# Attention on one Trainium2 core: the result kept transposed up to the output projection, normalised on GpSimd with sums turned through DRAM

## The reference

```
B, S, D, H, HD = 8, 1024, 256, 16, 16
h    = layernorm(x) * (1 + ca) + sa                    # modulation from silu(c) @ wmod
q    = h @ W_q;  latent = (h @ W_k + h @ W_v) @ W_down_kv
k, v = latent @ W_up_k, latent @ W_up_v                # 16 heads of 16
s    = (q_h @ k_h^T) / sqrt(D) * exp(-0.01 |t - t'|)
x    = x + ga * (softmax(s) @ v_h, heads joined) @ W_o
h    = layernorm(x) * (1 + cb) + sb
x    = x + gb * fp4_linear(silu(fp4_linear(h, w_gate)) * fp4_linear(h, w_up), w_down)
```

## Time and profile before

| | us |
|---|---|
| median of 3 runs | 2778.95 (2777.27 to 2779.09) |
| span of the profiled execution | 2775.7 |
| PE busy | 2597.7 (94%) |
| DVE busy | 2345.5 (85%) |
| ACT busy | 1601.3 (58%) |
| POOL busy | 970.2 (35%) |

### The profile page before, as it was taken

One profiled execution on the slowest core, in us unless ns is written; L12 is line 12 of the kernel. 1 busy time (PEld: TensorE's weight loads), 2 busy tenths in 40 slices (PEclk: granted clock), 3 DMA queues, 4 the chain that ended last, 5 costly groups with the idle time before them and its releaser, 6 DMA issues. The chain is left out here.

```text
span 2775.7 us, 54634 instructions
## 1 busy us (share of the span) xinstructions
PE 2597.7 (94%) x15110; PEld 1209.7 (44%) x15110; DVE 2345.5 (85%) x4659; ACT 1601.3 (58%) x2988; POOL 970.2 (35%) x865
## 2 busy tenths in 40 slices
PE   5887679999999999999999999999978999999998
PEld 3333213343444444344344344443323566666665
DVE  5888698888888888888888888888756999999997
ACT  3666507777777777777777777777762222222221
POOL 3666522122122122122122122122231555555654
PEclk8767659999999999999999999999997999999999
DMA  4777864446455455455456455456201111111110
GB/s 152 246 247 255 265 129 73 71 74 99 62 85 87 63 82 82 71 78 86 70 78 86 72 80 86 69 79 94 39 11 38 37 41 40 40 40 42 40 32 18
DMA packets 207121, 238.56 MB, mean 86 GB/s; under 512 B 32256, under 2 KB 150784, under 8 KB 206720
## 3 DMA queue, kind: packets, MB, share of 16 engines
q1 hardware_dynamic: 194560, 218.56, 40.7%
q0 software_dynamic: 3072, 8.39, 1.2%
q10 hardware_dynamic: 9216, 8.39, 0.9%
HBM read 149.79 MB, written 83.89 MB: 84 GB/s over the span
## 5 line engine op out<-in xcount | busy, mean ns | idle before, releaser
L856 DVE CUSTOM_DVE_ANT_0 unread<-max_ps,toeplitz_sb 128x1024 bf16<-128x1024 f32 x1024 | 1219.2, 1219 | 230.5 <-PE max_ps L689 221.9
L817 ACT ACTIVATE probs<-score_ps 128x512 f32<-128x512 f32 x2048 | 1113.3, 597 | 438.3 <-PE score_ps L722 299.7
L689 PE MATMUL max_ps<-k_low,q_low 96*128 96x512 bf16 x2048 | 717.5, 393 | 30.0 <-DVE ident_bf L847 17.9
L651 POOL TENSOR_TENSOR probs<-probs,up_probs 128x512 f32<-128x512 f32 x256 | 336.8, 1316 | 624.4 <-ACT up_probs L821 624.4
L750 PE MATMUL pv_ps<-probs,v 128*32 128x512 f32 x4096 | 548.9, 608 | 3.4 <-POOL probs L651 3.4
L722 PE MATMUL score_ps<-q_low,k_low 99*128 99x512 bf16 (+3 forms) x1280 | 407.9, 320 | 4.9 <-ACT probs L817 4.1
L714 PE MATMUL score_ps<-q_up,k_up 99*128 99x512 bf16 (+3 forms) x1280 | 408.0, 319 | 4.5 <-ACT probs L817 3.8
L1284 PE MATMUL gu_ps<-wgu_t,turned 128*128 128x512 f32 (+1 forms) x768 | 314.7, 559 | 0.6 <-DVE hid L1445 0.6
L657 POOL DMA_DIRECT2D attn<-out_n x64 | 48.8, 762 | 698.3 <-DVE out_n L920 674.8
L714 PEld LDWEIGHTS score_ps<-q_up,k_up 99*128 99x128 bf16 x1280 | 123.8, 97 | 350.4 <-ACT probs L817 325.2
L689 PEld LDWEIGHTS max_ps<-k_low,q_low 96*128 96x128 bf16 x2048 | 194.0, 99 | 156.5 <-DVE row_max L856 83.9
(11 more groups left out here) (145 smaller groups left out, 3218.2 us busy)
## 6 DMA issues: line engine op xcount, KB each, us to landing
splits<-parts SPq DMA_DIRECT2D x128, 384.0 KB, 2.6
q_low<-splits SPq DMA_DIRECT2D x192, 128.0 KB, 4.4
k_low<-splits SPq DMA_DIRECT2D x192, 128.0 KB, 7.0
q_up<-splits SPq DMA_DIRECT2D x192, 128.0 KB, 9.4
k_up<-splits SPq DMA_DIRECT2D x192, 128.0 KB, 12.0
v_padded<-v_out SPq DMA_DIRECT2D x64, 256.0 KB, 3.5
v<-v_padded SPq DMA_DIRECT2D x32, 512.0 KB, 13.9
x_in<-in_L_attn_x SPq DMA_DIRECT2D x16, 512.0 KB, 4.6
```

The costliest lines, as they stand in the source:

```text
L651: nc.gpsimd.tensor_tensor(probs[:, g % PROBS, :, at:at + P], probs[:, g % PROBS, :, at:at + P], up_probs[:, g % 2], ALU.add).then_inc(diag ...
L689: mm = pe.matmul(max_ps[:, i % 2, half * HALF:(half + 1) * HALF], low[0][u][0:KROWS, h, qb * P:(qb + 1) * P], low[1][u][0:KROWS, h, half * ...
L817: nc.scalar.activation(probs[:, g % PROBS, h, :], score_ps[:, i % 2, :], ACT.Exp).then_inc(exp_done, 1)
L856: nc.vector.tensor_tensor_reduce(unread[:, i % 2, :], max_ps[:, i % 2, :], toeplitz[:, at:at + S], 1.0, -3.0e38, ALU.mult, ALU.max, row_ma ...
```

## The change

The product of a half is no longer turned. `out_t` has two buffers, one a half. SP moves the four rows of sums to DRAM and back as 128 partitions x 16 (`turn_sums`), DVE inverts them there (`invert`, at the end of g = 6 for half 1 of the unit before, of g = 14 for half 0), SP moves the inverses to DRAM and back spread over all 32 rows of each head (`spread_inverse`), and POOL multiplies 128x512 in place (`normalise`: after its fourth diagonal addition for half 1 of the unit before, after its last for half 0). SP stores the result head by head to `attn_t` (four DMAs of 32 KB a half). The feed stage loads its tiles from `attn_t` as the left operand of the projection; its transposes of the attention result and that pipeline stage are gone.

```diff
@@ attention, SP
+        def turn_sums(b, u, hf):
+            n = 2 * (UNITS * b + u) + hf
+            sp.wait_ge(out_copied, n + 1)
+            sp.dma_start(t["sums"][hf], out_t[HD:P:VW, hf, :]).then_inc(sums_stored, 16)
+            sp.wait_ge(sums_stored, 16 * (n + 1))
+            sp.dma_start(sums[:, hf, :], t["sums"][hf].rearrange("h (a c) -> (h a) c", a=P // UH)
+                         ).then_inc(sums_loaded, 16)
+        def spread_inverse(b, u, hf):
+            n = 2 * (UNITS * b + u) + hf
+            sp.wait_ge(inverted, n + 1)
+            sp.dma_start(t["inverse"][hf].rearrange("h (a c) -> (h a) c", a=P // UH), inverse[:, hf, :]
+                         ).then_inc(inverse_stored, 16)
+            sp.wait_ge(inverse_stored, 16 * (n + 1))
+            sp.dma_start(inverse_rows[:, hf, :], t["inverse"][hf].unsqueeze(1).broadcast_to(
+                [UH, VW, HALF])).then_inc(inverse_loaded, 16)
+        def store_out(b, u, hf):
+            sp.wait_ge(out_normal, 2 * (UNITS * b + u) + hf + 1)
+            for h in range(UH):
+                sp.dma_start(t["attn_t"][b, u * UH + h, :, hf * HALF:(hf + 1) * HALF],
+                             out_t[h * VW:h * VW + HD, hf, :]).then_inc(out_stored[hf], 16)
         def step(b, u, last):
             ...
                 load_low(b if u < 2 else b + 1, (u + 2) % UNITS)
             if not (last and u == UNITS - 1):
                 load_up(b if u < UNITS - 1 else b + 1, (u + 1) % UNITS)
+            if not (isinstance(unit, int) and unit == 0):
+                before = (b if u > 0 else b - 1, (u - 1) % UNITS)
+                store_out(*before, 0)
+                turn_sums(*before, 1)
+                spread_inverse(*before, 1)
+                store_out(*before, 1)
+            turn_sums(b, u, 0)
+            if not (last and u == UNITS - 1):
                 load_max_rows(unit + 1, (u + 1) % UNITS)
+            spread_inverse(b, u, 0)
@@ attention, POOL
-            pool.dma_start(t["attn"][b, hf * HALF:(hf + 1) * HALF, ...], out_n[:]...)
+        def normalise(b, u, hf):
+            count = held(pool, 16 * (2 * (UNITS * b + u) + hf + 1))
+            pool.wait_ge(minus_ones_set, UNITS + 2)
+            pool.wait_ge(inverse_loaded, count)
+            nc.gpsimd.tensor_tensor(out_t[:, hf, :], out_t[:, hf, :], inverse_rows[:, hf, :],
+                                    ALU.mult).then_inc(out_normal, 1)
@@ attention, PE
-            for c in range(DIAG):
-                mm = pe.transpose(side_ps[:, c, :], out_t[:, c * P:(c + 1) * P], w["ident"][:])
-            mm.then_inc(out_turned, 1)
@@ attention, ACT
-            act.wait_ge(out_turned, n)
+            if not (isinstance(unit, int) and unit == 0):
+                act.wait_ge(out_stored[hf], 16 * OUT_STORES * unit)
@@ attention, DVE
-            nc.vector.reciprocal(inv_sum[:], turned[:, :, :, HD]).then_inc(inv_ready, 1)
-            nc.vector.tensor_tensor(out_n[:], turned[:, :, :, 0:HD], ...)
+            dve.wait_ge(sums_loaded, count)
+            nc.vector.reciprocal(inverse[:, hf, :], sums[:, hf, :]).then_inc(inverted, 1)
...
+                if g == 6 and not (isinstance(unit, int) and unit == 0):
+                    invert(b if u > 0 else b - 1, (u - 1) % UNITS, 1)
+                if g == 14:
+                    invert(b, u, 0)
@@ feed
-            sp.dma_start(attn_in[i % 4][:], t["attn"][b, i * P:(i + 1) * P, :]).then_inc(tile_loaded[i % 4], 16)
+            sp.dma_start(attn_in[i % 4][:], t["attn_t"][b, :, :, tokens].rearrange(
+                "(k h) d s -> (h d) k s", k=DC)).then_inc(tile_loaded[i % 4], 16)
-                mm = pe.matmul(out_ps[:, 0:D], turned[i % 2][:, k, :], w["wo_g"][:, b, k, :],
+                mm = pe.matmul(out_ps[:, 0:D], attn_in[i % 4][:, k, :], w["wo_g"][:, b, k, :],
-                mm = pe.transpose(turn_ps[:, k * P:(k + 1) * P], attn_in[i % 4][:, k * P:(k + 1) * P], w["ident"][:])
```

More of the change, by code:

```diff
@@ L636, in _ @@
             step(B - 1, u, True)
+        store_out(B - 1, UNITS - 1, 0)
+        turn_sums(B - 1, UNITS - 1, 1)
+        spread_inverse(B - 1, UNITS - 1, 1)
+        store_out(B - 1, UNITS - 1, 1)
+        for i in range(2):
+            sp.wait_ge(out_stored[i], 16 * OUT_STORES * UNITS * B)
     @block.gpsimd
@@ L724, in scores, with up_diagonals @@
             mm.then_inc(scores_ready, 1)
-        def up_diagonals(b, u, g):
+        def up_diagonals(b, u, g, last):
             unit, kb = UNITS * b + u, g % TILES
             ks = slice(kb * P, (kb + 1) * P)
-            if g == TILES + DIAG:
-                pe.wait_ge(out_ready, 2 * unit + 1)
+            if g == TILES + DIAG and not last:
+                pe.wait_ge(max_turn_copied, unit + 2)
             pe.wait_ge(up_limited, diagonals_before(unit, g))
@@ L775, in unit_steps @@
                     if h == 1 and is_diagonal(g):
-                        up_diagonals(b, u, g)
+                        up_diagonals(b, u, g, last)
                 if not (first and g < LAG):
                     values(*steps_back(b, u, g, LAG))
-                if g == 5 and not first:
-                    turn_out(2 * unit - 1)
                 if g == 9 and not last:
                     turn_maxima(unit + 1)
-                if g == 10:
-                    turn_out(2 * unit, 0 if last else unit + 2)
         def max_tiles(u, n):
@@ L804, in _, with copy_out @@
             values(B - 1, UNITS - 1, g)
-        turn_out(2 * UNITS * B - 1)
     @block.scalar
     def _(act):
-        def copy_out(n):
-            act.wait_ge(pv_done, TILES * (n + 1))
-            act.wait_ge(out_turned, n)
-            nc.scalar.activation(out_t[:], pv_ps[:], ACT.Copy).then_inc(out_copied, 1)
+        def copy_out(unit, hf):
+            act.wait_ge(pv_done, TILES * (2 * unit + hf + 1))
+            if not (isinstance(unit, int) and unit == 0):
+                act.wait_ge(out_stored[hf], 16 * OUT_STORES * unit)
+            nc.scalar.activation(out_t[:, hf, :], pv_ps[:], ACT.Copy).then_inc(out_copied, 1)
         def exp(unit, g, h):
@@ L908, in round_weights, with unit_steps @@
                               weight_scale).then_inc(weight_step, 1)
-        turned = side_ps[:].rearrange("p c (h r) -> p c h r", r=VW)
-        def invert_sums(n):
-            dve.wait_ge(out_turned, n + 1)
-            nc.vector.reciprocal(inv_sum[:], turned[:, :, :, HD]).then_inc(inv_ready, 1)
[L916 to L924, removed]
+        def unit_steps(b, u, last):
             unit = UNITS * b + u
@@ L931, in unit_steps @@
                         maxima(ahead[0], ahead[1], ahead[2] + i)
[L933 to L936, removed]
                     if not last and (g, i) in SPLIT_AT:
@@ L1158, in sem @@
         return st.enter_context(nc.semaphore(name))
-    attn_in = [sb(f"attn_in{i}", [P, D], F32) for i in range(4)]
+    attn_in = [sb(f"attn_in{i}", [P, DC, P], F32) for i in range(4)]
     res_in = [sb(f"res_in{i}", [P, D], F32) for i in range(4)]
-    turned = [sb(f"turned{i}", [P, 2 * DC, P], F32) for i in range(2)]
+    turned = [sb(f"turned{i}", [P, DC, P], F32) for i in range(2)]
     x1 = [sb(f"x1_{i}", [P, D], F32) for i in range(TILES)]
```

128 lines of the change are left out of this document (53 added, 75 removed).

## The result

The changed kernel takes 3028.43 us (median of 4 runs, 3011.67 to 3053.27) against 2778.11 (4 runs, 2773.45 to 2779.09): a ratio of 1.0906, 95% interval 1.0849 to 1.0963. The forecast was 2988, slower. Its profiled span is 3017.4, that of before 2775.7: +241.7 us to be explained.

What follows compares the result with a forecast made beforehand. PE's order of work was taken to bound both stages; waits 207 + clock 43 - `turn_out` 30 - feed 20 + end of attention 9 = +209 us on the 2775.7 span, 2985, so 2988 for the median; range 2905 to 3068.

Steps and rivals of the forecast that it cites:

- The deciding step: Half 1's sums wait behind SP's 25 loads (3.5 MB, first at T0); DVE waits about 9 us, PE loses 8.1.
- The other terms (26.4, 1.0 and 0.6): In us: burst ends at T0 + 26.4, four 32 KB stores add 1.0, landing of the sums' store adds 0.6.
- The term of the waits, 207: PE's loss in attention: 29 units of 8.1 us, less 28.2 us, makes 207 us.
- the extra after branches: 28.2 us by which units after a branch already ran long before g = 4, deducted whole from the waits.
- The step that failed is that on POOL: `normalise` for half 0 ends at T0 + 4.9, before the next unit's first addition at 5.6: costs nothing.
- rival (c): `normalise` for half 0 also holds the next unit's first addition: two us in 30 units, 3048 us; chance 0.06.
- The clock, 43: PE's clock drops after each wait: 1.8 us for each of 24 ordinary attention units, 43 us.
- Rival (b): The wait is there but PE's clock holds at 1.0: 2945 us; chance 0.13.
- `turn_out`, 30: PE in attention saves 63 `turn_out` at 0.47 us each inside the loop of units: 30 us.
- The end of attention, +9: From the last copy to the next stage's first load, 14.7 us in place of 5.7: +9.
- The feed stage, -20: PE loses two transposes a tile, 64 x 0.27 = 17 us, and pipeline filling 3 us: -20 us.
- Rival (a): The sums aren't held by the burst, so DVE never waits: -41, 2738 us; chance 0.11.

Runs made afterwards that it cites:

- experiments 1 and 2: 1: changed kernel, half 1's sums turned between the low and up loads, 2830.29 us; 2: changed kernel, half 1's reciprocal at the end of g = 9, 2845.47 us.
- experiment 12: Changed kernel with the inverses loaded in four loads of 64 KB, one a head: 2986.48 us, ratio 1.0749.
- experiment 8: Changed kernel with POOL's multiply for half 0 moved behind the next unit's fourth diagonal addition: 3024.96 us, ratio 1.0880.
- 11: Changed kernel with half 1's sums turned between the low and up loads, and the inverses in four loads, one a head: 2766.14 us, ratio 0.9952.
- experiment 10: Changed kernel, half 1's sums and half 0's stores before the up loads, half 1's stores after the maxima rows, POOL's half 0 multiply after the next unit's fourth addition: 2768.80 us.
- experiment 5: Changed kernel with 20 more PE matmuls (96x512, read by nobody) at the end of g = 7: 3031.86 us, ratio 1.0919.
- Experiments 6 and 7: 6: changed kernel, POOL's last hidden-rounding product on 160 of 704 columns, 3017.69 us; 7: changed kernel, DVE's rounding step 6 on 16 of 704, 3011.18 us.

## Why the prediction was right, and where it was off

**The deciding step held.** The sums queue behind SP's burst, DVE waits for them at the end of g = 6, PE behind DVE for the row maxima, the clock falls: all are in the rows above, and experiments 1 and 2 take the wait away by its place and by its reader. Over the 29 units the median time of the sums' load is T0 + 29.0 and of the reciprocal T0 + 30.8; predicted were 29.9 and 31.8. That this fits so well is partly luck. The prediction reached 29.9 with 1.9 us for the inverses' 256 KB at the burst's rate; in experiment 12, where these bytes are spread, the load of the sums comes at T0 + 25.8. The other terms (26.4, 1.0 and 0.6) were too long, and the undivided load's 3.2 us made up for it.

**The term of the waits, 207, was composed wrongly.** Measured idle time of PE is +184: 134 at `row_max` (136.0, less 2.2 in before), 41 at `values`, the rest of some 9 where the profile shows no releaser. A unit's wait of DVE is 165.1 / 29 = 5.7 us and not 9, or 8.1 with the extra after branches taken off. Of these 2.4 us, 1.4 are the reciprocal's earlier start (on average T0 + 30.4 in place of 31.8). The other 1.0 is DVE, which ends g = 6 later (on average T0 + 24.7 in place of 23.7 with that extra): PE, which feeds it, has stood at `values`. In experiment 8, without that wait, DVE ends g = 6 at T0 + 22.4, against 24.1 (medians). The step that failed is that on POOL, which said that the 256 KB for half 0 "land at about T0 + 3.5" and cost "nothing": POOL's multiply starts at T0 + 7.3. So rival (c), which was given 0.06, is there too, in small, but beside the forecast and partly in its place: experiment 8 takes the wait at `values` away and gains nothing measurable, because the sums' landing is fixed by the burst. The cause, shown by 11 and 12, is the undivided load, by its DMA share on a quarter of the engines. The prediction priced it by its bytes at the burst's rate, +1.9 us.

**The clock, 43, was too small.** Experiment 10 has the same instructions on PE as the changed kernel (x11055 and x11054) with hardly a wait: PE is busy 1509.8 us there and 1582.6 in the changed kernel. The same work thus costs 72.8 us more at a mean granted clock of 0.93 than at 0.99. The matmuls themselves say the same: one of 96x512 for the maxima takes 0.22 us of PE's time at the high level and 0.43 at the low one in both traces. Of PE's busy time some 180 us lie at the low level here and 31 in experiment 10; half of the difference is 75. In the unit with the long wait the first two steps after it cost 2.5 us over their usual length, not 1.8. All 29 units have the wait, not only the 24 for which the clock's price was counted. Rival (b) fell: the clock doesn't hold. A kernel with the wait but at full clock was not reached; experiment 5 left its time open.

**`turn_out`, 30:** right in size, 0.48 us against 0.47 each. In experiment 10 PE's busy time is 1534.6 - 1509.8 = 24.8 below that of before. So 184 + 72.8 - 24.8 = 232, the loss of the 30 units; predicted 207 + 43 - 30 = 220. That the two lie so close is luck in part: the waits were 23 too many, the clock 30 too little.

**The end of attention, +9:** the last copy starts at 2304.18 and the next stage's first load at 2320.15, 15.97 apart against 6.33 in the earlier trace rows: +9.6.

**The feed stage, -20, gave -1.9**, which is less than the stage differs between traces. PE lost its 0.27 us a tile, but a tile only went from 9.62 us to 9.60. The way of one tile in the changed kernel, in order of time, from the timelines of all engines:

```profile
2450.28 4.89 PE L1290 MATMUL gu_ps<-wgu_t,turned 128*128 128x512 f32 x12
...
2455.21 0.76 ACT L1322 ACTIVATE silu<-gu_ps 128x704 f32<-128x704 f32 x1 [3.87 <-PE gu_ps L1290]
...
2456.00 0.89 DVE L1442 TENSOR_TENSOR hid<-gu_ps,silu 128x704 f32<-128x704 f32 x1 [0.42 <-ACT silu L1322]
...
2463.61 0.88 DVE L1010 TENSOR_TENSOR hid_buf<-hid_buf 128x704 f32<-128x704 f32 x1
...
2465.49 1.68 POOL L1013 TENSOR_TENSOR hid_buf<-hid_buf 128x704 f32<-128x704 f32 x1
...
2467.24 1.39 POOL L1014 TENSOR_TENSOR hid<-hid_buf,hid_scale 128x704 f32<-128x704 f32 x1
...
2468.76 0.87 PE L1272 MATMUL hid_ps<-ident_sb,hid 128*128 128x128 f32 x6
2469.47 4.89 PE L1290 MATMUL gu_ps<-wgu_t,turned 128*128 128x512 f32 x12
```

`gate_up` releases `silu`, that DVE's product; DVE then rounds this hidden tile (among other steps, without a pause) until 2464.49, and POOL's part ends at 2468.63. PE's transposes of the tile begin 0.13 us later, and the last row, a `gate_up` again, stands behind them. The ring through all four engines thus takes 19.19 us and serves two tiles: 9.60 each. In the kernel before, with two more transposes ahead, those of the hidden tile began 0.24 us after POOL's product (median of the tiles); so of PE's 0.27 us only some 0.1 could be gained. The prediction read DVE's 5% of idle time as room; it was idle because it waited for `silu`. Experiments 6 and 7 shorten one member each and the stage falls by 7 and 16 us, so the ring bounds it. With both, the tile would by our estimate still end at PE's own floor of about 9.4 us (experiment 7: PE 397.8 of 400).

**The sum.** Forecast +209 on the span, measured +241.7: attention's units +12 over the forecast, feed +18, the start and end of the units' stretch some 2. The median of the runs is another 11.0 above the profiled span, where 3.2 were assumed. Rival (a) fell with SP's rows: the sums' load stands 18.2 us behind their store.

## What to carry to other kernels

A small round trip through DRAM cost here what stood ahead of it in its queue, not what it moves: list the queue in program order, and put the trip ahead of the burst that nobody waits for, with the stores that free a buffer. Look at a broadcast load's outermost dimension before pricing it by its bytes: the same 256 KB in four pieces were worth 64 us of 2830, and with the sums' place turned a loss of 9% into a gain of 0.5%. In a pipeline through several engines, an engine that is 95% busy need not have room in the other 5%; follow one tile through all engines until its ring closes, and see what the engine waits for.

## What the runs showed of the hardware that was not expected

- A load of 256 KB with an outermost dimension of 4 used 0.26 to 0.29 of the DMA engines at about 100 GB/s; POOL had it 5.2 us after its issue with nothing beside it (2310.24 to 2315.39), about 8 us with a burst behind it. In four loads of 64 KB each landed after a median of 2.0 us.
- 8 KB on another queue during the burst took 9.0 us, against 1.6 at a calm time, and landed with the burst's last load.
- The changed kernel's runs spread by 1.4%, those of before by 0.2%, those of experiments 10 and 11 again by 0.2 and 0.1%. Why was not tried. The long wait alone doesn't do it: in experiment 8, where DVE waits longest, the runs spread by 0.2%.
